# Moments of an MLP unit taken one step later, together with its normalising

## What is computed

```python
def _layer(x, wqkv, qs, ksc, wo, lg, lb, w1, b1, w2, b2):
    h = shift_token(x)
    q, k, v = heads(h @ wqkv)               # 8 heads of 64
    q, k = rotary_xpos(l2norm(q) * qs, l2norm(k) * ksc)
    o = local_attention(q, k, v)            # windows of 128, each with the window before it
    x = x + o @ wo
    h = shift_token(x)
    h = (h - h.mean(-1)) / jnp.sqrt(h.var(-1) + 1e-05) * lg + lb
    a, g = jnp.split(h @ w1 + b1, 2, axis=-1)
    return x + (a * gelu(g)) @ w2 + b2
```

## Time and profile before

| what | value |
|---|---|
| median of 3 runs | 5250.14 us (5248.26 to 5255.09) |
| the profiled execution: its own time | 5278.77 us |
| the profiled execution: span of its instructions | 5276.8 us |
| TensorE busy, share of the span | 81% |
| VectorE, ScalarE, GpSimd busy | 60%, 49%, 35% |
| mean granted TensorE clock | 0.902 of full speed |

### The profile page before, as it was taken

The page is one execution under the profiler, slowest core; times in us unless marked ns, Lnnn a source line. Parts: engine busy times, 40 slices in busy tenths (PEclk is TensorE's granted clock), DMA queues, the critical chain, the costliest instruction groups (busy, mean ns, idle before and its releaser), DMA issues. The chain is left out here.

```text
span 5276.8 us, 99786 instructions
## 1 busy us (share of the span) xinstructions
PE 4276.0 (81%) x33294; PEld 3110.8 (59%) x33294; DVE 3177.2 (60%) x7541; ACT 2580.7 (49%) x5522; POOL 1860.0 (35%) x1466
## 2 busy tenths in 40 slices
PE   4988988899858788787878878587878878787886
PEld 2454444554436666666666666466666666666665
DVE  5667776666546556475654646374655647566463
ACT  1555555555535455454544545354544545454453
POOL 3023232323214333343433434243434434343343
PEclk6899999998869999898998989798998989899998
DMA  5333444334110000000000000100000000000000
GB/s 133 76 73 85 97 107 107 69 79 104 41 66 11 13 14 12 16 11 13 14 11 17 9 15 10 63 16 20 18 16 18 14 22 16 20 18 16 22 14 19
DMA packets 148565, 200.27 MB, mean 38 GB/s; under 512 B 21708, under 2 KB 122536, under 8 KB 148016
## 3 DMA queue, kind: packets, MB, share of 16 engines
q1 hardware_dynamic: 148016, 193.19, 14.6%
HBM read 116.02 MB, written 67.68 MB: 35 GB/s over the span
## 5 line engine op out<-in xcount | busy, mean ns | idle before, releaser
L1050 DVE TENSOR_REDUCE a_mx<-a_ring 128x2 f32<-128x1024 f32 (+3 forms) x768 | 724.4, 956 | 278.2 <-PE a_ring L882 128.9
L728 ACT ACTIVATE a_e_t<-a_ring 128x1024 f32<-128x1024 f32 (+3 forms) x768 | 614.0, 809 | 566.2 <-PE a_ring L869 393.8
L1598 POOL TENSOR_TENSOR b_e<-b_e,b_share 128x512 f32<-128x512 f32 (+1 forms) x512 | 521.9, 1020 | 769.1 <-DVE b_share L2033 769.0
L1699 ACT ACTIVATE b_e<-b_e,b_bias 128x256 f32<-128x256 f32 (+1 forms) x1024 | 498.5, 488 | 602.0 <-DVE b_bias L2013 599.9
L1809 PE MATMUL b_bank_m<-b_h_t_hi,b_w_hi 128*128 128x256 f32 x1584 | 470.6, 297 | 89.1 <-issue 70.7
L1583 POOL TENSOR_TENSOR b_qk_rot<-b_qk_rot,b_rot 128x512 f32<-128x512 f32 x256 | 323.4, 1284 | 395.8 <-DVE b_rot L1987 395.8
L1809 PE MATMUL b_bank_m<-b_h_t_lo,b_w_hi 128*128 128x256 f32 x1584 | 458.7, 290 | 0.0
L1809 PE MATMUL b_bank_m<-b_h_t_hi,b_w_lo 128*128 128x256 f32 x1584 | 458.1, 289 | 0.0
L2109 DVE SCALAR_TENSOR_TENSOR b_ag<-b_bank_m,b_b_c,b_ag 128x256 f32<-128x256 f32 x396 | 191.4, 483 | 411.6 <-ACT b_ag L1727 409.7
L2013 DVE CUSTOM_DVE_ANT_0 b_e<-b_bank_s,b_mask,b_scale_q 128x256 f32<-128x256 f32 (+1 forms) x1024 | 432.6, 459 | 0.0
L1809 PE MATMUL b_bank_p<-b_wqkv_hi,b_turned_hi 128*128 128x512 f32 x768 | 366.0, 477 | 70.5 <-DVE b_turned_lo L2049 46.4
(11 more groups left out here) (229 smaller groups left out, 11075.6 us busy)
## 6 DMA issues: line engine op xcount, KB each, us to landing
a_q_st<-a_parts_q SPq DMA_DIRECT2D x192, 128.0 KB, 4.9
a_k_st<-a_parts_k SPq DMA_DIRECT2D x192, 128.0 KB, 7.4
b_fl<-f_rows SPq DMA_DIRECT2D x72, 256.0 KB, 4.0
a_parts_q<-a_qk_p SPq DMA_DIRECT2D x16, 1024.0 KB, 7.1
a_parts_k<-a_qk_p SPq DMA_DIRECT2D x16, 1024.0 KB, 8.1
a_xl<-in_L_attn_x SPq DMA_DIRECT2D x9, 1024.0 KB, 5.4
f_rows<-b_fr SPq DMA_DIRECT2D x33, 256.0 KB, 2.1
b_x_l<-x_rows SPq DMA_DIRECT2D x33, 256.0 KB, 3.0
```

Of the source, the lines that this page charges most:

```text
L728: act.activation(e_t[:, step % 2, 2 * pair:2 * pair + 2, 0:cols], slot[:, :].rearrange("p (h t) -> p h t", h=2)[:, :, 0:cols], ACT.Exp).th ...
L1050: dve.reduce_max(mx[:, g % 2, :, pair, piece, t:t + 1], slot[:, :].rearrange("p (r c) -> p r c", r=2)[:, :, 0:cols], AX.X)\
L1598: pool.tensor_tensor(weights, weights, share[:, pp, :].unsqueeze(2) .broadcast_to([P, 2, 2 * WIN - lo]), ALU.mult).then_inc(e_done.sem, 1)
L1699: ins = act.activation(weights, weights, ACT.Exp, scale=-1.0, bias=bias[:, pp, hh:hh + 1], accum_out=total[:, pp, hh:hh + 1])
```

## The change

For units 0, 1 and 2 the piece `moments` goes to the step of `norm`, one later. Since VectorE takes both pieces at the end of its step, moments and normalising now follow each other there. ScalarE's root for these units leaves its place ahead of the next step's exponentials and goes to the end of the step in which the moments are taken. Unit -1 stays as it was.

```diff
@@ plan_mlp
     for u, s in ((-1, FIRST), (0, 13), (1, 21), (2, 29)):
-        put(s, "moments", u, None)
+        put(s + int(u >= 0), "moments", u, None)
         put(s + 1, "norm", u, None)
         put(s + 2, "hT", u, None)
@@ ScalarE's body
                     for piece, u, m in pieces_at(pp - 1, closing):
-                        if piece == "moments":
+                        if piece == "moments" and u < 0:
                             piece_of_mlp(piece, u, m)
@@ ScalarE's body, end of the step
                     for x in pieces_at(pp, closing):
-                        if x[0] != "moments":
+                        if x[0] != "moments" or x[1] >= 0:
                             piece_of_mlp(*x)
```

## The result

The changed kernel takes 5199.55 us (median of 4, 5189.85 to 5206.36) against 5252.61 us before. The ratio is 0.9894, 95% interval 0.9875 to 0.9913: 1.06% faster, which is 53 us between the two medians and 56 us by the ratio (interval 46 to 66). 5176 was forecast. The range for 8 in 10, 5153 to 5222, held the time; the forecast's own range, 5160 to 5197, missed it by 3 us. The gain is about three quarters of the 74 us of the sum. Measured once more beside later experiments, the same kernel had a ratio of 0.9902 (0.9884 to 0.9920).

The account below looks back on a forecast made before the run. One late transfer, the shifted rows `b_hs`, was taken to stop three engines by being waited for ahead of ready work. Gains of 76.8 us less 3 gave 74, so 5250.1 would fall to about 5176; 8 in 10: 5153 to 5222.

Parts of the forecast that it names:

- the forecast's own range: Kernel time of 5160 to 5197 us, a gain of 53 to 90; the forecast's chance was 0.70.
- the 74 us of the sum: Whole kernel: 16 x (2.55 + 1.95 + 0.3) = 76.8 us for units 0, 1, 2, less 3 us of issue time.
- The late shift hid step 14's front part: VectorE ahead of the moments: 1.64 us of step 14 fits into the 1.77 us wait for `b_hs`, leaving about 0.1.
- Moments to end of norm, 3.60 us: VectorE, first BN_STATS to next step's start: 3.60 us in place of 5.27, priced from the last unit.
- The rival of a late root: ScalarE reaches the root behind late work; each unit loses 3.5 us, giving 5344 us; chance 0.04.
- The rival of the shared ports: GpSimd's scaling blocks VectorE's Newton step at shared SBUF ports, up to 1.04 us; held not to happen, no chance given.
- Step 15, 4.72 us: VectorE, start of step 15 to step 16 in units 0 and 1: 4.72 us at full clock, mean 5.25 before.
- The rival of the returning half clock: TensorE's idle times in step 15 bring back clock 0.50; 37 us lost, giving 5213 us; chance 0.13.
- The last `ag` matmul 11.7 us on: Step 16 to the last `ag` matmul: kept at 11.7 us, from 11.66 in the first unit.
- 0.4 us of issue time left in unit 0 of the first layer: Step 14 of unit 0: 0.4 of 0.47 us idle for issue stays in 8 samples, 3 us off the gain.
- Unit 2, +0.3 us: TensorE's idle time only moves to `b_hn` and the half clock reaches the `ag` matmuls; +0.3 us, bounds +0.9 and -0.9.
- No place holds the gain: Behind the unit, matmuls follow one another and loads and stores issue ahead, so no fixed time would take back the gain.

Follow-up runs that it names:

- VectorE's half alone: Against the kernel before, VectorE takes the moments of units 0 to 2 behind the later step's row maxima, ScalarE's root stays: 5256.23 us, ratio 1.0002.
- the two experiments on unit 2: Only unit 2 moved, against the kernel before: 5250.91 us, ratio 0.9998; the changed kernel with unit 2 a step later: 5150.66 us, ratio 0.9798.
- the added work: Changed kernel with two unused sums, about 1.2 us, ahead of the moments of units 0 to 2 on VectorE: 5263.04 us, ratio 1.0017 to before.

## Why the prediction was right, and where it was off

- **The late shift hid step 14's front part.** Right. The residual wait was put at 0.1 us; the moments begin with no wait. The share of step 14 starts 0.31 us behind the scale of the scores, which was not foreseen and costs next to nothing: the moments of the units 0 begin 4.60 to 4.62 us behind the issue of the shift, before it was 4.44 to 4.61. One reading was not quite right: the 64 waits of the earlier trace rows aren't four in each of 16 samples. Of 66 sets of moments the two of the last units after the samples are among them, and the first unit -1 of each layer isn't; the sum doesn't use this.
- **Moments to end of norm, 3.60 us.** Right: 3.59 to 3.61 in all units 0 and 2 and in unit 1 of the first layer, and the next step begins at 3.51. In unit 1 of the second layer it is 3.86; there the second Newton operation starts 0.29 us late behind the first, for a reason that no row shows. The row of the last unit was the right price, because both have nothing else ahead of the root. The rival of a late root fell: ScalarE idles 0.73 us or more ahead of it. The rival of the shared ports fell too: the first Newton operation takes 0.16 us in all 48 units, and took 0.74 to 0.82 in units 0 and 1 and 0.41 in unit 2 before.
- **Step 15, 4.72 us.** Right in all 32 units. The rival of the returning half clock fell: none was left in the stretches of 30 of the 32 units 0 and 1, and 3.4 us of it in the other two. VectorE's half alone shows how much hangs on it.
- **The last `ag` matmul 11.7 us on.** Right: 11.71 to 11.79 on average.
- **0.4 us of issue time left in unit 0 of the first layer**, 3 us: wrong, none is left (3.51 there too).
- **Unit 2, +0.3 us.** Mis-sized: its stretch is 0.1 us shorter in one execution of the changed kernel, 0.3 longer in the other and 0.4 shorter when it moves alone, which gives a ratio of 0.9998. The mechanism (the idle time moves, the half clock reaches into the `ag` matmuls) was right, and the two experiments on unit 2 show it from both sides.
- **No place holds the gain.** This is the step that failed, and the main reason why 74 us became 53 to 56. The stretches gave 72 us, but 13 of them were given back between the units, so the layers gained 59, and 60 in the second execution. The time at half clock from the moments of unit -1 to the end of its `ag` matmuls was 13.4 and 11.5 us before and 16.8 and 10.8 after (first and second layer), 16.4 and 17.0 when the changed kernel ran again, so part of it may be the clock; what ties it to the change is not shown. With units 0 and 1 alone moved the layers gain 66 of 69 us, and with unit 2 alone none of 6. In these single executions it is the move of unit 2 that goes with what is lost; the medians are too close to tell.
- **The range.** The bounds of the forecast's own range, unit 2 at +0.9 or -0.9 and 0.4 us either way on 32 others, give gains of 42 to 96 us when they are added up; it says 53 to 90, so it takes them as not falling together. The measured 53 to 56 lies at that edge.
- **The start.** The sum was made on the profiled execution and carried to the median unchanged. The profiled executions then went from 5278.8 to 5202.7 us where about 5205 was forecast, and that closeness is luck: 18 of the 76 us came from the stage ahead of the layers. Profiled executions differ by what the clock grants in the attention stage alone: the first moments of the layers began at 1545.8 us in the kernel before, at 1528.1 and 1538.0 in two executions of the changed kernel. That is why one pair of spans shows 76 us and the runs show 51 to 56.

That ScalarE as well as VectorE must be let past the late transfer is shown by VectorE's half alone, where the one further difference of order follows from leaving ScalarE as it was. That VectorE's moments and norm are on the path after the change is shown by the added work, paid in full within the noise.

## What to carry to other kernels

Ask of each wait in an engine's fixed order what stands ready behind it: a transfer that is late by 2 us cost nothing once the work behind it on two engines was put in front, and moving it on one engine alone only gave the stop to the next operand. In this kernel a gain on TensorE's side came in two parts, the idle time and the half clock behind it; a long idle time that only moved (unit 2) gave neither. When a change works, look for the same pattern at its neighbours: unit 2 and unit -1 together held more than the change itself had brought. For a change near 1% compare the stage that was changed, and not the whole span of two profiles.

## What the runs showed of the hardware

- Two idle times of TensorE of 1.1 to 1.5 us each within 5 us left the granted clock at 1.00 in 30 of the 32 units 0 and 1 of one execution and in 31 of 32 of another. Single ones of 2.6 to 4.3 us went with a clock of 0.50, during them or right behind, in all 48 units of the kernel before. Behind one of 2.3 to 2.4 us it fell in 16 of 32 units.
- One program's identical first stage ended up to 27 us apart between executions (the first moments at 1519.0 to 1545.8 us in kernels that differ only behind it), with 256 to 344 us at half clock in it. For a change of 1%, a pair of profiles is not enough.
- A VectorE operation of 0.16 us took 0.75 when it met a GpSimd instruction and ended with it. The Trainium skill (SBUF — State Buffer, Who interferes with whom) gives the rule, and the trace agrees on both sides: with GpSimd's scaling done before it, it takes 0.16, in all 48 units.
